# A four-layer graph network on one core: fourteen pairs of attention rows gathered beside the edges' scoring, two weight matrices loaded in the pass

## The reference, cut to what matters

```python
h = (x @ W.T).reshape(n, h_, d_)
h_src = h[src]
e = leaky_relu(einsum(h_src, a_src) + einsum(h[dst], a_dst), 0.2)
e = e * (1.0 + et_emb[edge_type]) * edge_weight[:, None]
e_max = zeros((n, h_)).at[dst].max(e)
e = exp(e - e_max[dst])
alpha = e / (zeros((n, h_)).at[dst].add(e)[dst] + 1e-10)
out = zeros((n, h_, d_)).at[dst].add(h_src * alpha[:, :, None])
```

## Time and profile before

| | us |
|---|---|
| median of three runs | 1920.26 |
| profiled execution | 1923.38 |
| its span, first to last instruction | 1921.6 |
| scoring, 954.0 to 1093.9 | 139.9 |
| attention weights, 1093.9 to 1138.8 | 44.9 |
| attention pass, 1138.8 to about 1360 | 221 |

### The profile page before, as it was taken

One profiled execution on the slowest core, in us unless ns is written; L12 is line 12 of the kernel. 1 busy time (PEld: TensorE's weight loads), 2 busy tenths in 40 slices (PEclk: granted clock), 3 DMA queues, 4 the chain that ended last, 5 costly groups with the idle time before them and its releaser, 6 DMA issues. The chain is left out here.

```text
span 1921.6 us, 27696 instructions
## 1 busy us (share of the span) xinstructions
PE 1604.0 (83%) x7565; PEld 978.1 (51%) x7566; DVE 1159.0 (60%) x2290; ACT 478.3 (25%) x894; POOL 736.1 (38%) x625
## 2 busy tenths in 40 slices
PE   6754975776498999998888629998499899999998
PEld 5751642334343555554455515554246545874486
DVE  5768968985455777776477776665675732122222
ACT  3301112432211555554345320000121111001200
POOL 0000887887084776661000147777661010000000
PEclk9997988999689999999989659999799999999999
DMA  0007854004901666673279327777305102430034
GB/s 25 0 20 285 280 162 121 1 1 131 345 29 60 208 202 186 187 177 68 92 281 366 129 75 209 210 209 199 85 1 156 58 1 89 150 111 1 1 137 135
DMA packets 76346, 248.96 MB, mean 130 GB/s; under 512 B 14901, under 2 KB 28582, under 8 KB 68346
## 3 DMA queue, kind: packets, MB, share of 16 engines
q1 hardware_dynamic: 38618, 147.08, 21.2%
q0 software_dynamic: 34592, 96.87, 18.9%
q10 hardware_dynamic: 3072, 4.20, 0.8%
HBM read 215.93 MB, written 32.00 MB: 129 GB/s over the span
## 5 line engine op out<-in xcount | busy, mean ns | idle before, releaser
L664 POOL DMA_INDIRECT tab_slots<-slot_words,slot_address x160 | 238.3, 1489 | 246.2 <-issue 235.5
L693 POOL DMA_INDIRECT e_rows<-tab_h,idx_h x176 | 178.9, 1017 | 292.7 <-POOLq L50 218.8
L1447 PE MATMUL dense_pY<-weights,dense_xT_block 128*128 128x512 f32 x640 | 284.2, 600 | 6.7 <-ACT dense_xT_block L1435 6.7
L1513 PE MATMUL dense_pY<-parts,dense_number 128*128 128x512 f32 x1000 | 235.5, 397 | 0.0
L994 POOL DMA_INDIRECT e_rows<-tab_q,idx_q x192 | 183.1, 954 | 98.7 <-issue 39.5
L787 PE MATMUL e_pS<-e_rows,e_onehot_ring 128*128 128x512 f32 x352 | 194.8, 644 | 21.4 <-DVE e_rows L763 19.2
L1513 PEld LDWEIGHTS dense_pY<-parts,dense_number 128*128 128x128 f32 x1000 | 187.7, 188 | 46.5 <-issue 1.4
L1447 PEld LDWEIGHTS dense_pY<-weights,dense_xT_block 128*128 128x128 f32 x640 | 120.9, 193 | 149.0 <-issue 140.4
L1067 PE MATMUL e_pS<-e_rows,e_onehot_f 128*128 128x512 f32 x384 | 181.6, 596 | 0.0
L877 PE MATMUL count_pA<-count_onehot_d,count_onehot_s 128*128 128x512 f16 (+1 forms) x576 | 116.9, 350 | 62.9 <-DVE count_onehot_d L855 59.3
L763 DVE TENSOR_TENSOR e_rows<-e_rows,e_pW 128x1024 f32<-128x1024 f32 x88 | 107.3, 1220 | 67.7 <-DMA e_rows<-tab_h,idx_h 67.6
(11 more groups left out here) (314 smaller groups left out, 2413.2 us busy)
## 6 DMA issues: line engine op xcount, KB each, us to landing
basis_piece<-in_L_gnn_basis_pieces SPq DMA_DIRECT2D x32, 2048.0 KB, 7.8
dense_number<-tab_edges_from SPq DMA_DIRECT2D x20, 1280.0 KB, 5.5
tab_edges_from<-counts_turned SPq DMA_DIRECT2D x10, 1280.0 KB
tab_edges_to<-counts_total SPq DMA_DIRECT2D x10, 640.0 KB
dense_number<-tab_edges_to SPq DMA_DIRECT2D x10, 640.0 KB, 6.0
tab_w<-basis_wout ACTq DMA_DIRECT2D x128, 32.0 KB
weights<-tab_w SPq DMA_DIRECT2D x4, 1024.0 KB, 6.6
weights<-in_L_gnn_W_T SPq DMA_DIRECT2D x3, 1024.0 KB
```

Source lines behind the costliest of these rows:

```text
L664: pool.indirect_dma_start(self.table, bass.IndirectOffsetOnAxis(self.address[:, t:t + 1], 0), self.words[:, t, :], None).then_inc(self.pla ...
L693: pool.indirect_dma_start(self.rows[:, q, s, :], None, self.table, bass.IndirectOffsetOnAxis(self.idx[:, j * 2 + s:j * 2 + s + 1], 0)).the ...
L1447: ins = self.nc.tensor.matmul(self.banks.at(self.bank(b, w)), self.xt[:, b % 2, c, :], weights[:, c, :], start=c == 0, stop=c == 3)
L1513: ins = self.nc.tensor.matmul(self.banks.at(self.first + b), self.number[:, self.slot(b), r * NB + k, :], self.parts[r][n][:, k, :], start ...
```

## The change

The row ring gets six more places for the first eight pairs alone: the halves of the three weight buffers, lent until pairs 0 to 5 have been read (pair 0 in the first half of `W[0]`, pair 5 in the second half of `W[2]`). Pairs 6 and 7 go to their own places 6 and 7, and pairs 8 to 13 to places 0 to 5, which are now free. All fourteen pairs, 28 indirect DMAs, are issued in `edge_scores` from its start, without a wait. The pass gathers pairs 14 to 87 under the same rule as before: pair j waits for pair j-8. The two matrices can no longer be loaded in `attention_weights`, since `W[0]` and `W[1]` hold rows; SyncE loads them in the pass, after pairs 0 to 5 are done.

```diff
-    def __init__(self, nc, ctx, name, table, idx):
+    def __init__(self, nc, ctx, name, table, idx, lent):
...
+        self.got_lent = [sem(f"got_lent{q}") for q in range(len(lent))]
+        self.early = len(lent) + BODYP
+
+    def is_lent(self, i, u):
+        return is_first(i) and u < len(self.lent)
+
+    def rows(self, i, u):
+        return self.lent[u] if self.is_lent(i, u) else self.ring[:, u, :, :]
+
+    def wait_got(self, eng, i, u):
+        if self.is_lent(i, u):
+            eng.wait_ge(self.got_lent[u], 32)
+        else:
+            eng.wait_ge(self.got[u], (i + (0 if u < len(self.lent) else 1)) * 32)
...
 attention_pass:
-            for j in range(BODYP, PAIRS):
+            for j in range(ring.early, PAIRS):
                 pool.wait_ge(summed, j + 2 - BODYP)
                 ring.gather(pool, j)
+
+        @block.sync
+        def _(sp):
+            sp.wait_ge(summed, len(ring.lent) + 1)
+            for tile, source in fetches:
+                sp.dma_start(tile, source).then_inc(fetched, 16)
+            sp.wait_ge(fetched, 16 * len(fetches))
...
 edge_scores:
+        @block.gpsimd
+        def _(pool):
+            for j in range(ring.early):
+                ring.gather(pool, j)
...
 attention_weights:
-        @block.sync
-        def _(sp):
-            for tile, source in weights:
-                sp.dma_start(tile, source).then_inc(weights_in, 16)
-            sp.wait_ge(weights_in, 16 * len(weights))
-
-        @block.gpsimd
-        def _(pool):
-            for j in range(BODYP):
-                ring.gather(pool, j)
```

More of the change, by code:

```diff
@@ L681, with attention_pass @@
 class RowRing:
-    def __init__(self, nc, ctx, name, table, idx):
-        self.nc, self.table, self.idx = nc, table, idx
+    def __init__(self, nc, ctx, name, table, idx, lent):
+        self.nc, self.table, self.idx, self.lent = nc, table, idx, lent
         sem = stage_semaphores(nc, ctx, name)
-        self.rows = ctx.enter_context(nc.sbuf_tensor(f"{name}_rows", [P, BODYP, 2, D], F32))
+        self.ring = ctx.enter_context(nc.sbuf_tensor(f"{name}_rows", [P, BODYP, 2, D], F32))
         self.got = [sem(f"got{q}") for q in range(BODYP)]
+        self.got_lent = [sem(f"got_lent{q}") for q in range(len(lent))]
[9 more added lines that the diff above has]
+            eng.wait_ge(self.got[u], (i + (0 if u < len(self.lent) else 1)) * 32)
     def gather(self, pool, j):
-        q = j % BODYP
+        i, u = j // BODYP, j % BODYP
         for s in range(2):
-            pool.indirect_dma_start(self.rows[:, q, s, :], None, self.table,
+            pool.indirect_dma_start(self.rows(i, u)[:, s, :], None, self.table,
                                     bass.IndirectOffsetOnAxis(self.idx[:, j * 2 + s:j * 2 + s + 1], 0)
-                                    ).then_inc(self.got[q], 16)
-def attention_pass(nc, name, C, ring, loc, block_turn, block_bank, block_end, acc, weight, side):
+                                    ).then_inc(self.got_lent[u] if self.is_lent(i, u) else self.got[u], 16)
+def attention_pass(nc, name, C, ring, loc, block_turn, block_bank, block_end, acc, weight, side, fetches):
     ns = H + 1
@@ L704, in attention_pass @@
         sem = stage_semaphores(nc, ctx, name)
-        rows, got = ring.rows, ring.got
+        rows = ring.rows
+        fetched = sem("fetched")
         ohr = sb("onehot_ring", [P, 4, 2, P], F32)
@@ L760, in multiply @@
             def multiply(i, u):
-                v.wait_ge(got[u], (i + 1) * 32)
-                r = rows[:, u, :, :].rearrange("p s (h d) -> p s h d", h=H)
+                ring.wait_got(v, i, u)
+                r = rows(i, u).rearrange("p s (h d) -> p s h d", h=H)
                 nc.vector.tensor_tensor(
@@ L786, in step @@
                     for s in range(2):
-                        nc.tensor.matmul(flat(pS[:, bass.ds(bank[u], 1), :]), ohr[:, u % 4, s, :], rows[:, u, s, :],
+                        nc.tensor.matmul(flat(pS[:, bass.ds(bank[u], 1), :]), ohr[:, u % 4, s, :], rows(i, u)[:, s, :],
                                          start=False, stop=True, skip_group_check=True)
@@ L1776, in edge_scores @@
 def edge_scores(nc, name, C, identb, est, edt, src_lo, src_block, loc, pair_block, es_out, ed_out,
-                basis):
+                basis, ring):
     U = 4
@@ L1930, with attention_weights @@
 L = SLOTS // PAIRS * P
-def attention_weights(nc, name, C, es, ed, factor, loc, block_f, wt, weights, ring):
+def attention_weights(nc, name, C, es, ed, factor, loc, block_f, wt):
     with ExitStack() as ctx:
@@ L1960, in attention_weights @@
         sem = stage_semaphores(nc, ctx, name)
-        weights_in = sem("weights_in")
         s_dve, scored_ready, laid, seq_out, first_out = (
@@ L2298, in gnn @@
         until_dense = ExitStack()
-        ring = RowRing(nc, until_dense, "e1", tab["h"], idx["h"])
+        ring = RowRing(nc, until_dense, "e1", tab["h"], idx["h"], [W[n // 2][:, n % 2 * 2:n % 2 * 2 + 2, :] for n in range(6)])
         with ExitStack() as ctx:
             es, ed = (ctx.enter_context(nc.sbuf_tensor(f"edge_{n}", [P, SLOTS, H], F32)) for n in ("e_src", "e_dst"))
-            edge_scores(nc, "scores", C, identb, est, edt, src_lo, src_block, loc["dst"], pairs["dst"], es, ed, basis[2])
+            edge_scores(nc, "scores", C, identb, est, edt, src_lo, src_block, loc["dst"], pairs["dst"], es, ed, basis[2],
+                        ring)
             attention_weights(nc, "att", C, es, ed, factor, loc["dst"][:, :], block_of_pair[:, :],
-                              wt, [(W[n][:, :, :], turned_rows(ins, name, 0))
-                                   for n, name in enumerate(("L2_gnn_W_neigh", "L2_gnn_W_self"))], ring)
+                              wt)
         attention_pass(nc, "e1", C, ring, loc["dst"], block_turn, block_bank, block_end, acc, wt,
-                       side)
+                       side, [(W[n][:, :, :], turned_rows(ins, name, 0))
+                              for n, name in enumerate(("L2_gnn_W_neigh", "L2_gnn_W_self"))])
         until_dense.close()
```

## The result

The changed kernel takes **1927.7 us** in the median of 20 runs (1922.73 to 1932.25), the kernel before 1920.76 (1916.78 to 1925.85): a ratio of 1.0033 with a 95% interval of 1.0025 to 1.0041. It is slower by a third of a per cent, about 7 us, where 6.4 were forecast.

A forecast was written before the change was run, and what follows sets the result against it. GpSimd's issue of its last gather was taken to bound the pass, the basis pieces' loads to be on the scoring's path. Pass -1.4, gathers +6.2 and clock +1.6 gave +6.4 us, median 1926.7, range 1919.0 to 1935.0.

The forecast's parts named there:

- The sum: Whole kernel: -1.4 + 6.2 + 1.6 = +6.4 us, median 1926.7; the forecast had chance 0.50.
- Pass, -1.4: Pass: 12 fewer gathers save 15.0 us, a later stream start costs 13.6, so the last issue comes 1.4 us earlier.
- Matrices in the pass, 0: Pass: the two matrices, 2.1 MB, load after pair 5 for 5.2 us of the DMA engines; costed at nothing.
- Attention weights, 0: Attention weights: 16 gathers and two loads go, but VectorE's chain sets the stage; costed at 0.
- Gathers in the scoring, 6.2: Scoring: 28 gathers need 18.2 us of the DMA engines, 12.0 fit in empty time, 6.2 delay the pieces' loads.
- Clock, 1.6: Scoring: TensorE's waits bring two drops to 1.2 GHz, 0.8 us each, 1.6 us together.
- The first rival: Scoring: pieces keep most of the engines, packets taken in turn; net +2.9, 1923.2, no change; chance 0.27 with all-gathers-fit case.
- The second rival: Scoring: gathers are served first at 0.89 us each, 12.9 us plus 2.7 for the clock; net +14.2, 1934.5; chance 0.18.
- The third rival: Attention weights: GpSimd had held VectorE's chain, 12.1 us come back; net -9.2, 1911.1, faster; chance 0.05.
- the marks named beforehand: Signs: last gather 1 to 2 us earlier, later first row wait, pieces landing above 7.8, scoring 146 to 150, attention weights 44.9.

The follow-up runs named there:

- e5: From e1: the fourteen places turn as one ring through the whole pass, loops written out, matrices loaded at the dense layers' start; 1909.16 us, ratio 0.9942; again 1913.41.
- e1: From the changed kernel: ten pairs gathered in the scoring after the mixing, four beside the attention weights; 1924.33 us, ratio 1.0023 to the kernel before.
- e7: From the kernel before: only the two matrices' load moves, from beside the attention weights to the pass after pair 6; 1920.31 us, ratio 0.9997.
- e8: From the changed kernel: ten pairs gathered at the start of the scoring, four after the mixing; 1923.39 us, ratio 1.0015 to the kernel before.

## Why the prediction was right

**The sum** was right to 1 us, 1926.7 against 1927.7, and slower was the side given the most. That it was so close is in part luck: the gathers' term was 2 us larger than the waits it stood for, and about as much came from variation in the scoring (1.0) and from the dense layers (0.9), which the sum did not have. Its terms:

- *Pass, -1.4: measured -1.9*, and -1.5 on average over the runs with either pass. 15.0 saved and 13.6 lost by the later start were 15.6 and 13.1. The mechanism is shown by e5: with the wait for pair 0 instead of pair 6 the same 148 gathers end the pass 12.5 us sooner than in e1, on which it is built. In that run the matrices moved as well, but by e7 their place is worth nothing in the pass.
- *Matrices in the pass, 0: right.* They were issued at 1167.72, 19.1 us into the pass (forecast 19.6), and landed after 5.5 and 8.3 us; e7 shows no cost.
- *Attention weights, 0: right*, +0.04.
- *Gathers in the scoring, 6.2: 4.2 are seen as waits.* That bytes in front of the pieces' loads cost what does not fit into empty time held, and so did the price of a gather (0.65 forecast, 0.68 measured). The empty time was larger than forecast: 14.8 us and not 12.0 by the change's waits, 12.1 by e8's.
- *Clock, 1.6: measured 1.6*, the number by luck. There were two waits with two slow steps each, less the one of before; the forecast had two drops beside that of before, each with one slow step.

**The first rival** gave the gathers one packet for each of the pieces' packets, some 20% of the busy time. Its time, 1923.2, was too low, but its rule is what the trace shows. The queues from 965 to 969 us, when both have work, from 971 to 977, when the buffers are taken and no piece can be loaded, and from 988 to 992, when both have work again:

```profile
q1 hardware_dynamic: 88, 1.44, 84.0%
q0 software_dynamic: 87, 0.29, 17.9%
```

```profile
q0 software_dynamic: 704, 2.31, 101.6%
```

```profile
q1 hardware_dynamic: 84, 1.38, 80.2%
q0 software_dynamic: 82, 0.27, 16.4%
```

Where both have work, one packet of the gathers went through for each of the pieces, which are larger, and the gathers had 16 to 18% of the engines' time. Where the pieces had none, the gathers had all of it. Over the whole of 975 to 994 the counts are 904 against 288: that is an average over loads and the gaps between them, and no share. The Trainium skill says ("DMA: Bandwidth & Descriptors", section "Queues, rings and completion order") that an engine goes round the queues that have work, a packet from each. The trace agrees, 88 against 87. The rival's 4.3 us of waits (4.6 less the 0.3 to spare) are near the 4.2 measured; what it left out is the clock, 1.6. It had the last 14 gathers ride on seven pieces. In fact four pieces were slowed, by up to 3.0 us each, and the gathers went on in the gaps between the loads, from 994 to 996 with 101.7% of the time.

**The second rival**, the gathers served first at 0.89 us each, is out on both counts. Pieces and gathers took turns, and a gather's time was 0.68. The 0.89 was read where a gather comes every 1.25 us. From 971 to 977, when several were waiting and nothing else was, 101.6% of 6 us for 704 packets are 0.69 us a gather: what lowered it was not the loads beside it.

**The third rival** is out by the stage itself: with GpSimd idle VectorE's chain takes the same time, and a scan 4.42 us as before.

Of the marks named beforehand the last gather came 2.5 us earlier (1 to 2 forecast; 1.8 on average over the runs with either pass); the others held.

**Left open** is the +0.90 of the dense layers. They lie between 538.5 and 540.1 us in these runs. In the change TensorE's first eight multiplications with the matrices, shortly after 22.4 us of waiting, ran at 1.2 GHz for longer than before (before, then the change):

```profile
1383.13 5.47 PE L1447 MATMUL dense_pY<-weights,dense_xT_block 128*128 128x512 f32 x8 [0.68 <-ACT dense_xT_block L1435]
```

```profile
1391.13 6.02 PE L1469 MATMUL dense_pY<-weights,dense_xT_block 128*128 128x512 f32 x8 [0.68 <-ACT dense_xT_block L1457]
```

That is 0.55 of the 0.90. This row takes 5.43 to 6.54 us in these runs, and goes with the stage's length: the granted clock over it is 0.66 before and 0.60 in the change, so it rises sooner or later after the same start. Why it rose later in every run that moves the matrices' load out of the attention weights was not settled; the load itself had landed long before in e7.

## What to carry to other kernels

A prefetch into a ring that is bound by the rate of its issuer is worth the issues that it takes away only if the issuer's next one does not wait longer in exchange: look at what the first issue that is left waits for, and let spare places turn in the ring instead of serving once. Spare transfer time is a quantity: count the empty microseconds of the DMA engines ahead of a load on the path, and see that what fills them is through when that load begins. To learn how two queues share the engines, take a stretch in which both have work; counts over loads and gaps together mislead. A stage's last stretch is not free either, if the barrier behind it then has to wait for what was issued there.

## What the runs showed of the hardware that was not expected

- Two queues with packets of different size (about 16.4 KB against 3.3 KB each) were served one packet to one where both had work: 88 against 87, 84% against 18% of the engines' time.
- A barrier of all engines behind GpSimd's gathers opened 5.1 us after its last issue had begun in e1 (a gather lands 4.0 us after its issue there), though no instruction of the stage waits for the rows.
- A wait of TensorE of 2.0 to 2.9 us for a piece was followed by two steps at 1.2 GHz, 1.0 and 0.2 to 0.3 us longer than the others.
- 28 gathers with 64 bytes a row took 3.3% of the DMA engines' time in 48 us and disturbed nothing that can be measured.
